# Four low parts move from VectorE to GpSimd: the folded key weights in a three-layer decoder kernel

## The chip, the cores and the metric

The kernel runs on one core of one Trainium2 chip. The metric is device time in microseconds of one execution. A core has five engines with a queue each: TensorE (PE in the profile; its weight loads are the row PEld), VectorE (DVE), ScalarE (ACT), GpSimd (POOL) and SyncE (SP), which here only issues DMAs. GpSimd's operations in this kernel read and write SBUF alone; VectorE and ScalarE also read PSUM, where TensorE's results land.

## The reference

Three layers follow one another on x of 16 x 512 tokens by 256 channels: a linear attention whose state is a product of two summed outer products, a cross attention with 16 heads of 64 channels over 64 context rows per batch entry, and a mixture of eight experts with relu. Each ends in a residual sum and a layer norm. The change lies in the second:

```python
q = x @ Wq.T
kv = context @ Wkv.T
k, v = jnp.split(kv, 2, axis=-1)
...
sim = jnp.einsum('bhid,bhjd->bhij', q, k) * SCALE
...
sim = jnp.where(mask[:, None, None, :], sim, max_neg)
attn = jax.nn.softmax(sim, axis=-1)
out = jnp.einsum('bhij,bhjd->bhid', attn, v)
out = out.transpose(0, 2, 1, 3).reshape(B, Nq, HEADS * DIM_HEAD)
return out @ Wout.T + b_out
```

## The kernel before

After a set-up phase that makes keys and values of all batch entries, the attention phase takes some 900 us and the experts the rest. The change touches the attention phase alone. It walks over 16 batch entries ("batches") with four slots each, one slot per tile of 128 tokens; a steady batch takes 54.9 us. Each engine has its own program for a slot (`pe_slot`, `act_slot`, `dve_slot`, `pool_slot`, `sp_slot`) and runs its instructions strictly in the written order; semaphores, waited for through `need`, are all that ties the engines to each other.

Products that need precision are made in three passes: each operand is held as a rounded high part (`_hi`) and the rest (`_lo`), and `three_passes` multiplies hi by hi, hi by lo, lo by hi.

The key weights of a batch are folded into one matrix A of 256 x 1024 (`a_hi`, `a_lo`): rows are x1's channels, columns the 16 heads times 64 context rows, so that a tile's `sim` is x1 times A. TensorE forms A for the next batch in slot 3 of the present one, in four pieces A0 to A3 of 128 x 512, each in one of two PSUM banks `pw0` and `pw1` that all the small products of a batch share in turn. The table `ORDER` says in which slot and place each is made: A0 and A1 at place a (between the tile's two halves of `sim`), SW at b, A2 at b, A3 at c, SB at d, ROW and M at e. In slot 3 TensorE's sequence is: sim half 0, A0, A1, sim half 1, the transposes of x1 (`tr`), SW, A2, four transposes of the probabilities (`pt`), the product z, A3, four more transposes, those of x, SB, the first half of the output product (`ob`), ROW, M, its second half. Then slot 0 of the next batch begins with sim half 0, which needs all of A.

A name in `SPLIT` is taken out of its bank twice: ScalarE copies it to the high part (`prep_hi`), VectorE subtracts that from the bank to give the low part (`prep_split`), and with this the bank is free. A name in `COPIED` is taken once, by ScalarE (`prep_copied`). `prep_done` picks the semaphore, and `number` its count.

GpSimd makes in each slot the inverse deviations (`rstd`, `nmr`) of the layer norms, adds biases to x1 and x (`xb`), multiplies the probabilities by 1/sum (`prob<-prob,rz`, two halves), and in slot 3 forms the low part of the values, `v_lo`. SyncE writes the mask into row 0 of `a_hi` in slot 0, once A2 is split, since A0 and A2 hold that row.

Of the kernel before, what the change touches and what calls it, by code (L numbers as in the profile page):

```python
# [20 lines left out]
ACT = mybir.ActivationFunctionType  # L21
# [6 lines left out]
P = 128  # L28
# [4 lines left out]
def f32(ap):  # L33
    return ap.bitcast(F32)
# [101 lines left out]
def setup_and_attention(nc, t, k, first, kv_scr, x2_scr, out_rows,  # L136
                        NB, S, C, NKV, MC, TPB, PAIRS, KEYS, HEADS, CAP):
    HK = KEYS // 2
# [44 lines left out]
    s = {n: k.sem(n) for n in (  # L183
        "x_loaded", "k_loaded", "v_loaded",
        "prep_made", "prep_hi", "prep_split", "prep_copied", "state_ready", "st_prod", "r_prod", "r_sum",
        "v_hi_made", "v_lo_made",
        "xT_made", "xT_hi", "xT_taken", "x1T_made", "x1T_hi", "x1T_taken", "xb_ready",
        "z_made", "z_taken", "x1_ready", "x1_biased",
        "sim_made", "max_made", "sim_taken", "exp_made", "sum_made", "rz_made", "p_ready",
# [19 lines left out]

    NAMES = [n for n, _, _ in ORDER]  # L210

    COPIED = ("G", "GT", "R", "SW", "SB")
    SPLIT = ("A0", "A1", "A2", "A3", "B0", "B1", "B2", "B3", "M", "MW", "ROW")
    FINISHED = SPLIT + ("T0", "T1", "ST")

    def number(it, name, kinds=NAMES):

        names = [n for n in NAMES if n in kinds]
        if isinstance(it, int):
            return (sum(enabled(n, i) for i in range(-2, it) for n in names)  # L220
                    + sum(enabled(n, it) for n in names[:names.index(name) + 1]))
        before = sum(enabled(n, i) for i in range(-2, 0) for n in names)
        return it * len(names) + before + names.index(name) + 1
# [4 lines left out]
    def prep_done(eng, it, name):  # L228

        if name in COPIED:  # L230
            need(eng, "prep_copied", number(it, name, COPIED))
        else:
            need(eng, "prep_split", number(it, name, FINISHED))
# [21 lines left out]
    def within(b):  # L255
        return not isinstance(b, int) or 0 <= b < NB

    def need(eng, name, value):

        if not isinstance(value, int) or value > 0:  # L260
            eng.wait_ge(s[name], value)
# [5 lines left out]
    def sp_slot(sp, it, slot, e):  # L267
        if slot == 0 and within(it):

            prep_done(sp, it - 1, "A2")  # L270
            mask_of = maskrow[0:1, it * NKV:(it + 1) * NKV] if isinstance(it, int) else maskrow[0:1, bass.ds(it * NKV, NKV)]
            sp.dma_start(f32(a_hi[0:1, 0, :]).rearrange("p (g j) -> p g j", j=NKV),
                         mask_of.unsqueeze(1).broadcast_to([1, HEADS, NKV])).then_inc(s["mask_in_a"], 16)
        if slot == 0 and within(it + 1):

            if within(it):
                need(sp, "prep_made", number(it - 1, "A3"))
            load_kv(sp, kraw, 0, it + 1, "k_loaded")
        if slot == 1 and within(it + 1):

            need(sp, "v_lo_made", it + 1)
            load_kv(sp, vraw, 1, it + 1, "v_loaded")
        if slot == 3 and within(it + 3):

            need(sp, "xT_made", 4 * (it + 2))
            need(sp, "xb_ready", 4 * (it + 2))
            need(sp, "x_loaded", 16 * (it + 3))
            sp.dma_start(xraw[:, (e + 1) % 2, :, 0:C], x_tiles(it + 3)).then_inc(s["x_loaded"], 16)
        n = 4 * it + slot
        if tile_exists(n - 2):  # L290
            store(sp, n - 2, (slot - 2) % 4, x2, "x2_ready", "x2_stored", x2_scr)
            store(sp, n - 2, (slot - 2) % 4, o_sb, "out_ready", "out_stored", out_rows)
# [129 lines left out]
    def pe_sim(pe, it, slot, h):  # L422

        n = 4 * it + slot
        need(pe, "sim_taken", 2 * n + h - 1)
        if h == 0:
            need(pe, "x1T_taken", n + 1)
            if slot == 0:
                prep_done(pe, it - 1, "A3")
                need(pe, "mask_in_a", 16 * (it + 1))  # L430
        for m in range(MC):
            last = three_passes(pe, sim[h][:, :], (x1T_hi[:, slot, m, :], x1T_lo[:, slot, m, :]),
                                (half(a_hi, h)[:, m, :], half(a_lo, h)[:, m, :]), m == 0, m == MC - 1)
        last.then_inc(s["sim_made"], 1)
# [78 lines left out]
    def prep_views(name):  # L513

        pw = pws[bank_of(name)]
        i = int(name[-1]) if name[-1].isdigit() else 0
        by_m = lambda buf: buf.rearrange("p (m e) -> p m e", m=MC)
        if name == "G":
            return pw[:, 0:2 * C + 2 - P], g_sb[:, :], None
        if name == "GT":  # L520
            return pw[:, 0:P], g10[:, :], None
        if name == "R":
            return pw[:, 0:C], s_bc[:, :], None
        if name == "SW":
            return by_m(pw[:, :]), sw[:, :, :], None
        if name == "SB":
            return by_m(pw[:, 0:MC * P]), sbd[:, :, :], None
        if name == "ROW":
            return pw[0:1, :], rows[0:1, :], rows[32:33, :]
        if name == "M":  # L530
            return by_m(pw[:, :]), mmw_hi[:, :, 0:C], mmw_lo[:, :, 0:C]
        if name == "MW":
            return by_m(pw[:, :]), mmw_hi[:, :, C:2 * C], mmw_lo[:, :, C:2 * C]
        if name[0] == "A":
            return pw[:, :], half(a_hi, i // 2)[:, i % 2, :], half(a_lo, i // 2)[:, i % 2, :]
        return (pw[:, :].rearrange("p (r c) -> p r c", r=2), b_hi[:, 2 * i:2 * i + 2, :],
                b_lo[:, 2 * i:2 * i + 2, :])

    def act_prep(act, name, it):
        if name in COPIED + SPLIT:  # L540
            src, dst, _ = prep_views(name)
            need(act, "prep_made", number(it, name))
            act.activation(dst, src, ACT.Copy).then_inc(s["prep_hi" if name in SPLIT else "prep_copied"], 1)

    def act_norm(act, ln, q, src, dst, done):
# [186 lines left out]
    def pool_rstd(pool, ln, n, q):  # L732

        counted[f"mv{ln}"].wait_next(n + 1)
        pool.tensor_scalar(ve[:, q, ln:ln + 1], mv[:, ln, q, 1:2], EPS, None, ALU.add).then_inc(s[f"ve{ln}"], 1)
        pool.wait_ge(s[f"ve{ln}"], n + 1)

        need(pool, ("z_taken", "x1_ready")[ln], n - 1)
        pool.tensor_tensor(rstd[:, q, ln:ln + 1], ve[:, q, ln:ln + 1], epsc[:, 0:1], ALU.pow).then_inc(s[f"rstd{ln}"], 1)
        if ln:  # L740
            counted[f"rstd{ln}"].wait_next(n + 1)
            pool.tensor_scalar(nmr[:, q, ln:ln + 1], mv[:, ln, q, 0:1], rstd[:, q, ln:ln + 1], -1.0,  # L742
                               ALU.mult, ALU.mult).then_inc(s[f"nmr{ln}"], 1)
# [25 lines left out]
    def pool_state(pool, it):  # L769
# [4 lines left out]
        pool.tensor_tensor(sbdT[:, :, :], sprod[:, :, :], blockmask[:, :].unsqueeze(1).broadcast_to([P, MC, P]),  # L774
                           ALU.mult).then_inc(s["state_ready"], 1)

    def pool_slot(pool, it, slot, e):
        par = lambda a: (e + a) % 2
        has_sim, has_z, has_prev, has_xT, has_x1T = parts(it, slot)
        n = 4 * it + slot  # L780
        q = slot % 2
        if tile_exists(n - 2):
            pool_rstd_twice(pool, n - 2, q)
        if slot == 3 and within(it + 1):
            need(pool, "v_hi_made", it + 2)
            pool.tensor_tensor(v_lo[:, :, :], vraw[:, :, :], f32(v_hi[:, :, :]), ALU.subtract).then_inc(s["v_lo_made"], 1)
        if has_x1T:

            need(pool, "x1T_made", n + 4)
            x1_tile = x1[:, par(1 if slot else 0), (slot - 1) % 4, 1:C + 1]  # L790
            pool.tensor_tensor(x1_tile, x1_tile, boutbc[:, :], ALU.add).then_inc(s["x1_biased"], 1)
        if has_z:
            pool_rstd(pool, 0, n + 4, q)
        if slot == STATE_SLOT and within(it + 2) and not (isinstance(it, int) and it == -2):
            pool_sums(pool, it)
        if has_xT:

            pool_xb(pool, n + 5, it + 1 if slot < 3 else it + 2, (slot + 1) % 4, par(1 if slot < 3 else 2))
        if has_sim:
            need(pool, "rz_made", n + 1)  # L800
            for h in range(2):
                part = by_head(prob[:, q, h * HK:(h + 1) * HK])
                pool.tensor_tensor(part, part, rz[:, q, h * 8:h * 8 + 8].unsqueeze(2).broadcast_to([P, 8, NKV]),  # L803
                                   ALU.mult).then_inc(s["p_ready"], 1)
        if slot == STATE_SLOT and within(it + 2) and not (isinstance(it, int) and it == -2):
            pool_state(pool, it)
        if has_z:
            pool_rstd(pool, 1, n + 4, q)
# [30 lines left out]
    x1T_lo = k.sb("x1T_lo", [P, TPB, MC, P], F32R)  # L839
    a_hi = k.sb("a_hi", [P, MC, KEYS], F32R)  # L840
    a_lo = k.sb("a_lo", [P, MC, KEYS], F32R)
    b_hi = k.sb("b_hi", [P, PAIRS, C], F32R)
    b_lo = k.sb("b_lo", [P, PAIRS, C], F32R)
    v_hi = k.sb("v_hi", [P, PAIRS, P], F32R)
# [750 lines left out]
```

## Time and profile before

| | |
|---|---|
| three runs | 1389.42, 1390.56, 1391.6 us; median 1390.56 |
| the profiled execution | 1389.46 us, its span 1387.7 us |
| busy, share of the span | PE 95%, PEld 84%, DVE 65%, ACT 39%, POOL 44% |
| granted TensorE clock | 0.982 on average, 1.00 in the steady batches |

The profiled execution ends 1.76 us after its span and lies 1.10 us under the median. A timeline row gives the start in us from the start of the span, the duration in us, engine, line, operation, output and inputs; brackets give the engine's idle time ahead of it and what ended that.

### The profile page before, as it was taken

To read this page: it belongs to the slowest core of one execution; us is meant where nothing else is said; L and a number is where in the kernel's file an instruction comes from. 1 tells how busy PE (TensorE), PEld (TensorE's weight loads), DVE (VectorE), ACT (ScalarE), POOL (GpSimd) and SP (SyncE) were. 2 spreads that over 40 slices of the span, in tenths; PEclk is the share of its full clock that TensorE was granted. 3 is DMA by queue.
4 is the path that set the end of the run, shared out by engine and by line. 5 is a ranking of instruction groups with operands and counts; after the bars stand their busy time and mean duration, and the time that the engine had idled before them with its cause. 6 is when DMAs were issued, how large, how long until landed. Compare 5 with 4: busy or idle time off the path is not lost. (4 is left out here: it accounts for less than half of the span.)

```text
span 1387.7 us, 24816 instructions
## 1 busy us (share of the span) xinstructions
PE 1315.2 (95%) x8276; PEld 1161.0 (84%) x8276; DVE 897.2 (65%) x1762; ACT 541.8 (39%) x1041; POOL 604.8 (44%) x958
## 2 busy tenths in 40 slices
PE   7977999999999999999999999898589999999997
PEld 5766888888898888988888988787469988999897
DVE  5535878878878888788788887787434333223333
ACT  2013454454445454544544444344251233213321
POOL 2114656556466466565664665554331221122201
PEclk9999999999999999999999999999989999999999
DMA  8641011111111111111110101310121110111000
GB/s 266 145 97 31 24 39 39 43 35 47 30 46 36 33 46 38 39 38 30 46 45 23 54 32 39 115 31 24 31 62 61 62 36 26 60 60 60 0 0 31
DMA packets 117426, 69.46 MB, mean 50 GB/s; under 512 B 74081, under 2 KB 114786, under 8 KB 117346
## 3 DMA queue, kind: packets, MB, share of 16 engines
q1 hardware_dynamic: 114226, 66.81, 16.5%
q10 hardware_dynamic: 3120, 1.71, 0.4%
q8 instruction: 35, 0.57, 0.2%
q14 instruction: 45, 0.37, 0.1%
HBM read 42.22 MB, written 26.21 MB: 49 GB/s over the span
## 5 line engine op out<-in xcount | busy, mean ns | idle before, releaser
L1378 POOL TENSOR_TENSOR w_lo<-w_raw,w_hi 128x2048 fp32r<-128x2048 f32 x16 | 73.7, 4606 | 241.0 <-ACT w_hi L1329 192.5
L1351 ACT ACTIVATE hT_hi<-up 128x512 fp32r<-128x512 f32 x128 | 76.0, 597 | 236.2 <-PE up L133 236.2
L131 PE MATMUL ob<-b_hi,pT_hi 128*128 128x256 f32 x512 | 160.1, 313 | 6.6 <-DVE pT_lo L728 6.4
L803 POOL TENSOR_TENSOR prob<-prob,rz 128x512 f32<-128x512 f32 x128 | 130.9, 1043 | 66.9 <-DVE rz L690 66.9
L1540 DVE SCALAR_TENSOR_TENSOR hT_lo<-up,hT_hi 128x512 fp32r<-128x512 f32 x128 | 88.3, 691 | 96.6 <-ACT hT_hi L1351 96.6
L131 PE MATMUL dn<-w_hi,hT_hi 128*128 128x256 f32 x512 | 145.3, 284 | 0.8 <-DVE acc L1549 0.8
L133 PE MATMUL ob<-b_hi,pT_lo 128*128 128x256 f32 x512 | 145.2, 284 | 0.0
L133 PE MATMUL dn<-w_hi,hT_lo 128*128 128x256 f32 x512 | 145.1, 283 | 0.0
L132 PE MATMUL dn<-w_lo,hT_hi 128*128 128x256 f32 x512 | 145.1, 283 | 0.0
L132 PE MATMUL ob<-b_lo,pT_hi 128*128 128x256 f32 x512 | 145.1, 283 | 0.0
L547 ACT ACTIVATE x<-h,nmr,rstd 128x256 f32<-128x256 f32 x128 | 76.3, 596 | 116.7 <-POOL nmr L742 109.2
L1549 DVE SCALAR_TENSOR_TENSOR acc<-dn,coef,acc 128x256 f32<-128x256 f32 x64 | 30.9, 484 | 138.4 <-PE dn L133 138.4
L598 ACT ACTIVATE prob<-prob 128x512 f32<-128x512 f32 x128 | 80.7, 630 | 99.0 <-DVE prob L721 99.0
L131 PE MATMUL sim<-a_hi,x1T_hi 128*128 128x512 f32 x256 | 105.5, 412 | 6.1 <-DMA a_hi<-maskrow 6.1
L131 PEld LDWEIGHTS ob<-b_hi,pT_hi 128*128 128x128 f32 x512 | 98.1, 192 | 11.4 <-DVE pT_lo L728 8.0
L131 PE MATMUL up<-x2T_hi,w_hi 128*128 128x512 f32 x256 | 100.9, 394 | 1.5 <-POOL w_lo L1378 1.5
L132 PEld LDWEIGHTS ob<-b_lo,pT_hi 128*128 128x128 f32 x512 | 98.4, 192 | 3.3 <-issue 3.3
L132 PE MATMUL sim<-a_lo,x1T_hi 128*128 128x512 f32 x256 | 101.1, 395 | 0.0
L133 PE MATMUL sim<-a_hi,x1T_lo 128*128 128x512 f32 x256 | 100.6, 393 | 0.0
L132 PE MATMUL up<-x2T_lo,w_hi 128*128 128x512 f32 x256 | 100.5, 393 | 0.0
L133 PE MATMUL up<-x2T_hi,w_lo 128*128 128x512 f32 x256 | 100.3, 392 | 0.0
L131 PEld LDWEIGHTS dn<-w_hi,hT_hi 128*128 128x128 f32 x512 | 98.4, 192 | 1.3 <-DVE acc L1549 1.0
(218 smaller groups left out, 3591.6 us busy)
## 6 DMA issues: line engine op xcount, KB each, us to landing
xraw<-in_x SPq DMA_DIRECT2D x16, 512.0 KB, 4.0
kv_scratch<-stage SPq DMA_DIRECT2D x32, 256.0 KB, 2.6
x_scratch<-x SPq DMA_DIRECT2D x64, 128.0 KB, 1.7
out_x<-o_sb SPq DMA_DIRECT2D x64, 128.0 KB, 1.8
w_raw<-in_L_ffn_experts_inter SPq DMA_DIRECT2D x8, 1024.0 KB, 5.0
w_raw<-in_L_ffn_experts_out SPq DMA_DIRECT2D x8, 1024.0 KB, 7.5
kraw<-kv_scratch SPq DMA_DIRECT2D x32, 128.0 KB, 2.9
vraw<-kv_scratch SPq DMA_DIRECT2D x32, 128.0 KB, 3.0
```

The costliest lines, as they stand in the source:

```text
L131: pe.matmul(out, lh, rh, start=first, stop=False)
L132: pe.matmul(out, lh, rl, start=False, stop=False)
L133: return pe.matmul(out, ll, rh, start=False, stop=last)
L547: act.activation(dst, src, ACT.Identity, bias=nmr[:, q, ln:ln + 1], scale=rstd[:, q, ln:ln + 1]).then_inc(s[done], 1)
L598: act.activation(prob[:, q, h * HK:(h + 1) * HK], prob[:, q, h * HK:(h + 1) * HK], ACT.Exp).then_inc(s["exp_made"], 1)
L803: pool.tensor_tensor(part, part, rz[:, q, h * 8:h * 8 + 8].unsqueeze(2).broadcast_to([P, 8, NKV]), ALU.mult).then_inc(s["p_ready"], 1)
L1351: act.activation(hT_hi[:, h, i, :], up[i % 4][:, :], ACT.Relu).then_inc(s["up_hi"], 1)
L1378: pool.tensor_tensor(lo[:, u, :, :], raw[:, :, :], f32(hi[:, u, :, :]), ALU.subtract).then_inc(s["w_lo_made"], 1)
L1540: dve.scalar_tensor_tensor(hT_lo[:, h, i, :], up[i % 4][:, :], 0.0, f32(hT_hi[:, h, i, :]), ALU.max, ALU.subtract).then_inc(s["up_free"], 1)
L1549: dve.scalar_tensor_tensor(acc[:, i, :], dn[i % 2][:, 0:C], col, acc[:, i, :], ALU.mult, ALU.add).then_inc(s["dn_free"], 1)
```

## The change

A0 to A3 go from `SPLIT` to `COPIED`. ScalarE now reads each bank twice: it makes the high part as before, and right behind it a plain copy in a new SBUF buffer of two places, `a_raw`. GpSimd subtracts the high part from the copy (`pool_a_lo`). GpSimd's four subtractions stand in slot 3: A0 and A1 where `v_lo` stood, A2 between the first norm's `rstd` and `xb`, A3 behind the two multiplications of the probabilities, and `v_lo` behind A3. ScalarE waits ahead of each piece until GpSimd has taken the one before the last (the place in `a_raw`), and TensorE's sim of slot 0 and SyncE's mask wait for `a_lo_made` in place of `prep_split`.

```diff
-    COPIED = ("G", "GT", "R", "SW", "SB")
-    SPLIT = ("A0", "A1", "A2", "A3", "B0", "B1", "B2", "B3", "M", "MW", "ROW")
+    COPIED = ("G", "GT", "R", "SW", "SB", "A0", "A1", "A2", "A3")
+    SPLIT = ("B0", "B1", "B2", "B3", "M", "MW", "ROW")
...
-            prep_done(sp, it - 1, "A2")
+            need(sp, "a_lo_made", 4 * it + 3)
...
-                prep_done(pe, it - 1, "A3")
+                need(pe, "a_lo_made", 4 * (it + 1))
...
-            return pw[:, :], half(a_hi, i // 2)[:, i % 2, :], half(a_lo, i // 2)[:, i % 2, :]
+            return pw[:, :], a_raw[:, i % 2, :], half(a_hi, i // 2)[:, i % 2, :]
...
-            src, dst, _ = prep_views(name)
+            src, dst, hi = prep_views(name)
             need(act, "prep_made", number(it, name))
+            if name[0] == "A":
+                need(act, "a_lo_made", 4 * (it + 1) + int(name[1]) - 1)
+                act.activation(hi, src, ACT.Copy).then_inc(s["a_hi_made"], 1)
             act.activation(dst, src, ACT.Copy).then_inc(s["prep_hi" if name in SPLIT else "prep_copied"], 1)
...
+    def pool_a_lo(pool, it, i):
+
+        need(pool, "a_hi_made", 4 * (it + 1) + i + 1)
+        need(pool, "prep_copied", number(it, f"A{i}", COPIED))
+        pool.tensor_tensor(half(a_lo, i // 2)[:, i % 2, :], a_raw[:, i % 2, :], f32(half(a_hi, i // 2)[:, i % 2, :]),
+                           ALU.subtract).then_inc(s["a_lo_made"], 1)
+
...
-        if slot == 3 and within(it + 1):
-            need(pool, "v_hi_made", it + 2)
-            pool.tensor_tensor(v_lo[:, :, :], vraw[:, :, :], f32(v_hi[:, :, :]), ALU.subtract).then_inc(s["v_lo_made"], 1)
+        has_a = slot == 3 and within(it + 1) and not (isinstance(it, int) and it == -2)
+        if has_a:
+            pool_a_lo(pool, it, 0)
+            pool_a_lo(pool, it, 1)
...
         if has_z:
             pool_rstd(pool, 0, n + 4, q)
+        if has_a:
+            pool_a_lo(pool, it, 2)
...
+        if has_a:
+            pool_a_lo(pool, it, 3)
+            need(pool, "v_hi_made", it + 2)
+            pool.tensor_tensor(v_lo[:, :, :], vraw[:, :, :], f32(v_hi[:, :, :]), ALU.subtract).then_inc(s["v_lo_made"], 1)
```

GpSimd's rows in slot 3 of batch 0, from the last `nmr` of the output norms on, before:

```order
L756 TENSOR_SCALAR nmr<-rstd,mv 128x2
L786 TENSOR_TENSOR v_lo<-vraw,v_hi 128x1024
L791 TENSOR_TENSOR x<-x,boutbc 128x256
L735 TENSOR_SCALAR ve<-mv 128x1
L739 TENSOR_TENSOR rstd<-ve,epsc 128x1
L761 TENSOR_TENSOR xb<-xraw,bprime 128x256
L803 TENSOR_TENSOR prob<-prob,rz 128x512 x2
L735 TENSOR_SCALAR ve<-mv 128x1
L739 TENSOR_TENSOR rstd<-ve,epsc 128x1
L742 TENSOR_SCALAR nmr<-mv,rstd 128x1
```

And after (the line numbers are those of the changed kernel; L784 is `pool_a_lo`):

```order
L759 TENSOR_SCALAR nmr<-rstd,mv 128x2
L784 TENSOR_TENSOR a_lo<-a_raw,a_hi 128x512 x2
L802 TENSOR_TENSOR x<-x,boutbc 128x256
L738 TENSOR_SCALAR ve<-mv 128x1
L742 TENSOR_TENSOR rstd<-ve,epsc 128x1
L784 TENSOR_TENSOR a_lo<-a_raw,a_hi 128x512
L764 TENSOR_TENSOR xb<-xraw,bprime 128x256
L816 TENSOR_TENSOR prob<-prob,rz 128x512 x2
L784 TENSOR_TENSOR a_lo<-a_raw,a_hi 128x512
L821 TENSOR_TENSOR v_lo<-vraw,v_hi 128x1024
L738 TENSOR_SCALAR ve<-mv 128x1
L742 TENSOR_TENSOR rstd<-ve,epsc 128x1
L745 TENSOR_SCALAR nmr<-mv,rstd 128x1
```

`v_lo` has moved behind the multiplications, and four subtractions stand in the queue, one of them between `rstd` and `xb`, one between the multiplications and the next `rstd`.

ScalarE's rows in the same slot, from A0 to the first copy of the transposed probabilities (`pT_hi`), before:

```order
L543 ACTIVATE a_hi<-pw1 128x512
L543 ACTIVATE a_hi<-pw0 128x512
L547 ACTIVATE x1<-h1,nmr,rstd 128x256
L566 ACTIVATE v_hi<-vraw 128x1024
L598 ACTIVATE prob<-prob 128x512
L571 ACTIVATE x1T_hi<-tr 128x256
L543 ACTIVATE sw<-pw1 128x512
L543 ACTIVATE a_hi<-pw0 128x512
L604 ACTIVATE pT_hi<-pt 128x512
```

And after (L545 makes the high part, L546 the plain copy):

```order
L545 ACTIVATE a_hi<-pw1 128x512
L546 ACTIVATE a_raw<-pw1 128x512
L545 ACTIVATE a_hi<-pw0 128x512
L546 ACTIVATE a_raw<-pw0 128x512
L550 ACTIVATE x1<-h1,nmr,rstd 128x256
L569 ACTIVATE v_hi<-vraw 128x1024
L601 ACTIVATE prob<-prob 128x512
L574 ACTIVATE x1T_hi<-tr 128x256
L546 ACTIVATE sw<-pw1 128x512
L545 ACTIVATE a_hi<-pw0 128x512
L546 ACTIVATE a_raw<-pw0 128x512
L607 ACTIVATE pT_hi<-pt 128x512
```

Each `a_hi` is followed by an `a_raw`; x1's norm, `sw` and `pT_hi` stand one to three instructions further back. On VectorE four rows `a_lo<-pw,a_hi` are gone and nothing else moves.

## Rows read from the trace of the kernel before

**Rows 1.** The page's first part: busy time, share of the span, instructions of one engine.
```profile
PE 1315.2 (95%) x8276; PEld 1161.0 (84%) x8276; DVE 897.2 (65%) x1762; ACT 541.8 (39%) x1041; POOL 604.8 (44%) x958
```

**Rows 2.** Waits of PE from 150 to 945 us: total, times, longest.
```profile
PE sim L131 <- DMA a_hi<-maskrow: 6.1, 1, 6.1
PE tr L408 <- ACT x L547: 4.1, 10, 0.4
PE ob L131 <- DVE pT_lo L728: 1.4, 2, 1.3
```

**Rows 3.** Groups of instructions by shape: busy time and mean ns, idle time before.
```profile
L803 POOL TENSOR_TENSOR prob<-prob,rz 128x512 f32<-128x512 f32 x128 | 130.9, 1043 | 66.9 <-DVE rz L690 66.9
...
L1378 POOL TENSOR_TENSOR w_lo<-w_raw,w_hi 128x2048 fp32r<-128x2048 f32 x16 | 73.7, 4606 | 241.0 <-ACT w_hi L1329 192.5 <-ACT w_hi L1332 48.6
...
L614 DVE TENSOR_TENSOR a_lo<-pw,a_hi 128x512 fp32r<-128x512 f32 x64 | 43.7, 690 | 33.4 <-ACT a_hi L543 33.4
...
L786 POOL TENSOR_TENSOR v_lo<-vraw,v_hi 128x1024 fp32r<-128x1024 f32 x16 | 38.1, 2380 | 4.1 <-ACT v_hi L566 4.1
```

**Rows 4.** Timeline of ACT in slot 3 of batch 7; the last row is in slot 0 after it.
```profile
552.78 0.60 ACT L543 ACTIVATE a_hi<-pw 128x512 fp32r<-128x512 f32 x1 [0.30 <-PE pw L389]
553.79 0.60 ACT L547 ACTIVATE x<-h,nmr,rstd 128x256 f32<-128x256 f32 x1 [0.41 <-POOL nmr L742]
...
556.78 0.60 ACT L543 ACTIVATE a_hi<-pw 128x512 fp32r<-128x512 f32 x1 [0.17 <-PE pw L389]
557.27 0.59 ACT L604 ACTIVATE pT_hi<-pt 128x512 fp32r<-128x512 f32 x1
...
560.97 0.41 ACT L543 ACTIVATE sbd<-pw 128x256 f32<-128x256 f32 x1
...
569.28 0.59 ACT L547 ACTIVATE x<-h,nmr,rstd 128x256 f32<-128x256 f32 x1
```

**Rows 5.** Timeline of DVE in the same slot 3.
```profile
558.02 0.68 DVE L728 TENSOR_TENSOR pT_lo<-pt,pT_hi 128x512 fp32r<-128x512 f32 x1
...
559.40 0.18 DVE L647 BATCH_NORM_AGGREGATE mv<-bst 128x2 f32<-128x6 f32 x1
560.37 0.69 DVE L614 TENSOR_TENSOR a_lo<-pw,a_hi 128x512 fp32r<-128x512 f32 x1 [0.79 <-ACT a_hi L543]
...
562.30 0.25 DVE L690 RECIPROCAL rz<-zsum 128x16 f32<-128x16 f32 x1
```

**Rows 6.** Timeline of POOL in the same slot 3 and the slot after it.
```profile
555.28 0.27 POOL L756 TENSOR_SCALAR nmr<-rstd,mv 128x2 f32<-128x2 f32 x1 [0.19 <-POOL rstd L754]
555.51 2.38 POOL L786 TENSOR_TENSOR v_lo<-vraw,v_hi 128x1024 fp32r<-128x1024 f32 x1
...
559.75 0.22 POOL L735 TENSOR_SCALAR ve<-mv 128x1 f32<-128x1 f32 x1 [1.27 <-DVE mv L647]
...
560.59 0.74 POOL L761 TENSOR_TENSOR xb<-xraw,bprime 128x256 f32<-128x256 f32 x1
562.64 2.04 POOL L803 TENSOR_TENSOR prob<-prob,rz 128x512 f32<-128x512 f32 x2 [1.30 <-DVE rz L690]
...
565.83 0.27 POOL L742 TENSOR_SCALAR nmr<-mv,rstd 128x1 f32<-128x1 f32 x1 [0.19 <-POOL rstd L739]
```

**Rows 7.** Timeline of PE in the same slot 3: x1's transposes, ROW.
```profile
554.53 0.41 PE L408 MATMUL tr<-ident,x 128*128 128x128 f32 x2 [0.41 <-ACT x L547]
...
561.83 0.61 PE L366 MATMUL pw<-sbd,bq 128*128 128x128 f32 x4
```

**Rows 8.** Timeline of PEld: the first weight load of the next batch's slot 0.
```profile
565.35 0.19 PEld L131 LDWEIGHTS sim<-a_hi,x1T_hi 128*128 128x128 f32 x1
```

**Rows 9.** Timeline of PE in slots 0 of batches 14 and 15.
```profile
899.85 0.77 PE L131 MATMUL sim<-a_hi,x1T_hi 128*128 128x512 f32 x1 [6.10 <-DMA a_hi<-maskrow]
...
949.80 0.40 PE L131 MATMUL sim<-a_hi,x1T_hi 128*128 128x512 f32 x1
```

**Rows 10.** Timeline of POOL in slot 3 ahead of batch 15.
```profile
947.75 2.05 POOL L803 TENSOR_TENSOR prob<-prob,rz 128x512 f32<-128x512 f32 x2 [2.05 <-DVE rz L690]
```

More of the change, by code:

```diff
@@ L185, in setup_and_attention @@
         "prep_made", "prep_hi", "prep_split", "prep_copied", "state_ready", "st_prod", "r_prod", "r_sum",
-        "v_hi_made", "v_lo_made",
+        "v_hi_made", "v_lo_made", "a_hi_made", "a_lo_made",
         "xT_made", "xT_hi", "xT_taken", "x1T_made", "x1T_hi", "x1T_taken", "xb_ready",
@@ L841, in setup_and_attention @@
     a_lo = k.sb("a_lo", [P, MC, KEYS], F32R)
+    a_raw = k.sb("a_raw", [P, 2, HK])
     b_hi = k.sb("b_hi", [P, PAIRS, C], F32R)
```

## Prediction

> **What bounds the kernel now.** I read the page's busy shares first: PE is busy 95% of the span and DVE 65% [rows 1]. Then the waits of PE between 150 and 945 us, where the steady batches lie: the reader is to see how little is there. One wait of 6.1 us is for the mask of batch 14, which queues behind the experts' first weights; the rest is 4.1 us at x1's transposes and 1.4 us for VectorE's `pT_lo` [rows 2]. In 795 us PE stands still for 5.5 us besides the mask. So TensorE's stream is the bound, and VectorE, which the change relieves, holds it up for 1.4 us of it. A change of the copy engines can give back hardly anything, and it costs whatever it makes TensorE wait. The question is therefore one of due times in slot 3: which of the new instructions end after TensorE asks for them. I follow slot 3 of batch 7 (549 to 565 us); its rows repeat from batch to batch within some 0.1 us.
>
> TensorE asks for A at the first weight load of slot 0, at 565.35 [rows 8]. Before, VectorE had A3's low part done at 560.37 + 0.69 = 561.06 [rows 5], well ahead. Now it comes from GpSimd, and behind two multiplications that ended at 564.68 [rows 6].
>
> **What goes.** Four subtractions of 0.69 us on VectorE per batch [rows 3], 2.76 us. They lie under TensorE's work, so I cost their absence at nothing. What gets earlier is the softmax's chain: the reciprocal `rz` stood at 562.30 to 562.55 [rows 5], 1.24 us behind the end of A3's subtraction (the sum over the probabilities lies between). Now that sum can start at about 559.8, when the statistics of z are done (below), and `rz` is there near 559.8 + 1.24 + 0.25 = 561.3. GpSimd waited 1.30 us for it ahead of the multiplications [rows 6]; that gap is the cover for the new work, and it is used up below.
>
> **What ScalarE adds.** Four plain copies per batch. Two of its operations in a row start 0.49 us apart: A2's `a_hi` at 556.78 and `pT_hi` at 557.27 [rows 4]. The trace has no second copy of a bank, but this one waits for nothing, so 0.49 us is its price; the bounds are 0.49 and the full 0.60. The copy of A0 falls into the idle 0.30 us ahead of A1 and moves A1 by 0.09; A1's copy moves x1's norm, which waited 0.41 us for `nmr`, from 553.79 to 551.88 + 4 x 0.49 = 553.84 [rows 4]. TensorE waits for that norm already [rows 7], so this passes on: 0.05 to 0.06 us. A2's copy moves `pT_hi` by 0.55 to 557.82, A3's moves `sbd` by 0.55 from 560.97 to 561.52, done 561.93 [rows 4]; ROW's matmuls at 561.83 [rows 7] need it and start some 0.2 us late. This 0.2 is not added to the sum, because TensorE then waits that much less at slot 0.
>
> `pT_hi` ends at 558.41, so VectorE's `pT_lo`, at 558.02 before, starts at 558.46 and ends near 559.1. Behind it stands the statistics of z, and its aggregate of 559.40 [rows 5] becomes 559.62. GpSimd's `ve` waits for just that and goes from 559.75 to 559.97 [rows 6]. The subtraction that left VectorE from ahead of `pT_lo` gives nothing back, since the new copy on ScalarE is the longer way.
>
> **What GpSimd adds.** The trace has no 128x512 subtraction there. Rows of the same operation with two full inputs are 2.380 us for 1024 columns and 4.606 for 2048 [rows 3]: 2.17 ns a column and 0.15 us fixed, so 512 columns take 1.26 to 1.27. The bounds are 1.04, the 512 columns of `prob` whose second input is only 16 numbers wide over both halves [rows 3], and 1.48, twice the 0.74 of `xb` [rows 6]. I take 1.25. Operations in a row start 0.04 before the end of the one ahead, as `v_lo` and `nmr` show [rows 6].
>
> A0 and A1 take the place of `v_lo`, from 555.51: 2 x 1.25 against 2.38, over by 557.97. Then x1's bias, and GpSimd is waiting for z at 559.97 as before. Then:
>
> - `ve` to `xb` was 0.84 us [rows 6]: A2 starts at 560.81 and ends 562.06;
> - `xb` 562.02 to 562.76; the multiplications 562.72 to 564.76, against 564.68 before: A2 has used the 1.30 us of cover, and nothing is left for A3;
> - A3 564.72 to 565.97; with 0.05 for the semaphore TensorE may load at 566.02 instead of 565.35: 0.67 us of wait per batch.
>
> The Trainium skill, page "GPSIMD Engine Reference", section 4.1 "Engine selection", speaks against this step: elementwise work on a tile belongs on VectorE, GpSimd being about twice as slow with two inputs. Its section 3.1 gives 4497 ns for 2048 columns, where this trace has 4606 for a subtraction of that size. Taking a quarter, 1.12 us, as an estimate from that page, the wait would be about 0.4 and the sum 7 us; the rows above decide.
>
> What is queued behind A3: `v_lo` (2.38) and the norm that gives x1's `nmr`, whose end was 1.42 us after the multiplications' [rows 6]. With the 0.04 of overlap it comes 2.34 + 1.42 = 3.76 us after A3's end, at 569.73. x1's norm in slot 0 was at 569.28, 3.93 us after TensorE's start on that slot [rows 4, 8], as it stands behind MW on ScalarE; with the shift it is at 569.95. So this second wait is covered, by 0.2 us. SyncE's mask goes out when A2's low part is there, 562.1 in place of 560.4, and is needed at 566: covered.
>
> **The sum.** A is made in slot 3 of batches 0 to 14 and once ahead of batch 0. For 13 of them (made for batches 1 to 13) 0.67 each: 8.7 us. For batch 14 TensorE waits 6.10 us for the mask anyway [rows 9] and A3 is hidden; the weights that hold the mask up are issued behind a store that ScalarE's norms release, 0.55 later: 0.5. For batch 15 the multiplications end at 949.80 [rows 10], just when TensorE starts sim [rows 9]: 1.3. For batch 0 there are no multiplications, GpSimd is later all the same: 0.4, between 0 and 1. Together 10.9 us. The profiled execution took 1389.46, so 1400.4; the median of the runs is 1.10 above it, so 1401.5. I say 1401.
>
> **The rivals.**
> *Hidden or nearly so.* If a subtraction costs 1.04 (the lower bound), A3 ends 0.42 earlier, and if `pT_lo` does not hold up the statistics, another 0.22: 0.03 to 0.25 per batch, 1 to 4 us with the edges: 1391.5 to 1395. For it: the row of `prob` is of this very size. Against: both its inputs are not full tiles.
> *ScalarE becomes the bound.* It now also waits for GpSimd: A2's `a_hi` needs A0's place in `a_raw`, free at 555.51 + 1.25 = 556.76, and was made at 556.78 before [rows 4, 6]: no slack. If GpSimd is later by some tenths, `a_hi`, `pT_hi` and `pT_lo` follow, and TensorE's second four transposes, which need the bank that `pT_lo` reads, and ROW wait with them. With 1.48 per subtraction alone the wait at slot 0 is 0.67 + 2 x 0.23 = 1.13 per batch; with an estimated 0.3 on top, the size of the delays on ScalarE, it is 1.4: 1389.5 + 18 + 2 + 1, 1410 or more.
> *Faster.* VectorE's 2.76 us per batch come ahead of everything that feeds TensorE, the waits for `pT_lo` and for x1's norm shrink, and A3 is hidden by the lower bound. All there is to win is the 4.1 + 1.4 us of [rows 2] and some in the last slots: 1384 to 1387. It would decide from the point where A3's low part ends before 565.3. Against it: x1's norm in slot 3 waits for GpSimd's `nmr`, whose queue VectorE's relief, later in that slot, does not reach.
>
> **How the numbers follow.** My forecast (0.4 to 1.1 us per batch, 1395.5 to 1408) gets 0.62, for its order of work is fixed and only one price is unknown. Hidden or nearly so 0.20, of which 0.12 lies within 0.2% (2.8 us, 1387.8 to 1393.3, about what a measurement can tell) and 0.08 above. ScalarE as bound 0.08. Faster 0.10, of which 0.02 within 0.2%. So faster 0.08, same 0.14, slower 0.78. The range of 8 in 10 goes from 1392, which takes in the upper part of the hidden case, to 1408, the upper bound of the price.
>
> **What would show it.** Right: a wait of PE or PEld at sim's first load in slot 0 for POOL `a_lo` of about 0.5 to 0.7 us, some 13 times; `a_lo<-a_raw,a_hi` at 1.25; the multiplications in slot 3 with no wait for `rz`; VectorE 44 us less busy, ScalarE 30 to 38 more, GpSimd 80 more. Wrong: `a_lo` near 1.04 or below and no wait at sim; waits that move to `pt` or ROW for ScalarE; or x1's transposes waiting in slot 0 for `nmr` by more than before, since its cover is 0.2 us.

## The result, and the profile after

The changed kernel takes 1405.93 us (median of 4 runs, 1405.35 to 1406.84) against 1389.99 us before (4 runs, 1388.78 to 1391.6): a ratio of 1.0115, 95% interval 1.0097 to 1.0132. It is slower by 15.9 us, where the forecast had added 10.9 us and named 1401. The measured time lies inside the range of 1392 to 1408, in its upper part. Its profiled execution took 1405.35 us, with a span of 1403.6.

The page's first part answers to [rows 1]:

```profile
PE 1320.2 (94%) x8276; PEld 1159.9 (83%) x8276; DVE 861.8 (61%) x1698; ACT 568.2 (40%) x1105; POOL 683.1 (49%) x1022
```

VectorE is busy 35 us less, ScalarE 26 and GpSimd 78 more, and TensorE 5 us more in a span 16 us longer. The waits of PE between 150 and 960 us (total, times, longest), which answer to [rows 2]:

```profile
PE tr L408 <- ACT x L550: 7.8, 15, 0.6
PE sim L131 <- DMA a_hi<-maskrow: 6.5, 1, 6.5
PE sim L131 <- POOL a_lo L784: 3.1, 12, 0.4
PE ob L131 <- DVE pT_lo L731: 1.3, 1, 1.3
```

A new wait has come, for `a_lo` at the first sim of a batch, 12 times, and that for x1's norm at the transposes has grown from 4.1 to 7.8 us. The wait for `pT_lo`, which is VectorE's, has hardly moved, 1.4 to 1.3. These rows understate what is lost. In batch 7 the first sim shows a wait of 0.29 us on PE, and its row lasts 0.49 us where that of before lasts 0.40:

```profile
573.87 0.49 PE L131 MATMUL sim<-a_hi,x1T_hi 128*128 128x512 f32 x1 [0.29 <-POOL a_lo L784]
```

With the wait at x1's transposes (0.54 us after 0.41) the rows list 0.42 us more than before, while the slot became 0.95 us longer, as follows. So the distance between weight loads is the better measure. The groups that answer to [rows 3]:

```profile
L784 POOL TENSOR_TENSOR a_lo<-a_raw,a_hi 128x512 fp32r<-128x512 f32 x64 | 81.7, 1287 | 0.9 <-ACT a_raw L546 0.7 <-ACT a_hi L545 0.2
...
L546 ACT ACTIVATE a_raw<-pw 128x512 f32<-128x512 f32 x64 | 38.5, 601 | 0.0
...
L821 POOL TENSOR_TENSOR v_lo<-vraw,v_hi 128x1024 fp32r<-128x1024 f32 x16 | 38.2, 2389 | 0.0
```

Now batch 7 again. PEld's rows, where slot 3 begins (the first load of sim), x1's transposes, ROW, and the beginning of slot 0:

```profile
556.86 0.19 PEld L131 LDWEIGHTS sim<-a_hi,x1T_hi 128*128 128x128 f32 x1
...
562.20 0.20 PEld L408 LDWEIGHTS tr<-ident,x 128*128 128x128 f32 x2 [0.93 <-issue]
...
569.68 0.52 PEld L366 LDWEIGHTS pw<-sbd,bq 128*128 128x128 f32 x4 [0.20 <-ACT sbd L546]
...
573.87 0.19 PEld L131 LDWEIGHTS sim<-a_hi,x1T_hi 128*128 128x128 f32 x1 [0.49 <-issue]
```

Slot 3 lasts 573.87 - 556.86 = 17.01 us. Before, the rows of the same loads were these, with the end of the slot in [rows 8]:

```profile
549.29 0.19 PEld L131 LDWEIGHTS sim<-a_hi,x1T_hi 128*128 128x128 f32 x1
...
554.50 0.20 PEld L408 LDWEIGHTS tr<-ident,x 128*128 128x128 f32 x2 [0.80 <-issue]
...
561.72 0.53 PEld L366 LDWEIGHTS pw<-sbd,bq 128*128 128x128 f32 x4
```

That is 565.35 - 549.29 = 16.06 us, so this slot 3 costs 0.95. Counted from the start of the slot, x1's transposes come at 5.34 us, where they came at 5.21 before. ROW's first load comes at 12.82 after 12.43, later by 0.39, of which 0.13 stem from the transposes and 0.26 are new. The next sim comes at 17.01. ScalarE's rows, to be held against [rows 4]:

```profile
560.99 0.62 ACT L546 ACTIVATE a_raw<-pw 128x512 f32<-128x512 f32 x1
561.47 0.62 ACT L550 ACTIVATE x<-h,nmr,rstd 128x256 f32<-128x256 f32 x1
...
564.55 0.60 ACT L545 ACTIVATE a_hi<-pw 128x512 fp32r<-128x512 f32 x1 [0.25 <-PE pw L389]
565.05 0.59 ACT L546 ACTIVATE a_raw<-pw 128x512 f32<-128x512 f32 x1
565.53 0.61 ACT L607 ACTIVATE pT_hi<-pt 128x512 fp32r<-128x512 f32 x1
...
569.21 0.42 ACT L546 ACTIVATE sbd<-pw 128x256 f32<-128x256 f32 x1
...
577.77 0.59 ACT L550 ACTIVATE x<-h,nmr,rstd 128x256 f32<-128x256 f32 x1
```

VectorE's, against [rows 5]:

```profile
566.17 0.69 DVE L731 TENSOR_TENSOR pT_lo<-pt,pT_hi 128x512 fp32r<-128x512 f32 x1 [1.89 <-ACT pT_hi L607]
...
567.32 0.18 DVE L650 BATCH_NORM_AGGREGATE mv<-bst 128x2 f32<-128x6 f32 x1
...
568.73 0.25 DVE L693 RECIPROCAL rz<-zsum 128x16 f32<-128x16 f32 x1
```

and GpSimd's, against [rows 6]:

```profile
562.85 0.27 POOL L759 TENSOR_SCALAR nmr<-rstd,mv 128x2 f32<-128x2 f32 x1 [0.19 <-POOL rstd L757]
563.08 2.52 POOL L784 TENSOR_TENSOR a_lo<-a_raw,a_hi 128x512 fp32r<-128x512 f32 x2
...
567.68 0.22 POOL L738 TENSOR_SCALAR ve<-mv 128x1 f32<-128x1 f32 x1 [1.49 <-DVE mv L650]
...
568.52 1.29 POOL L784 TENSOR_TENSOR a_lo<-a_raw,a_hi 128x512 fp32r<-128x512 f32 x1
569.76 0.73 POOL L764 TENSOR_TENSOR xb<-xraw,bprime 128x256 f32<-128x256 f32 x1
570.44 2.06 POOL L816 TENSOR_TENSOR prob<-prob,rz 128x512 f32<-128x512 f32 x2
572.44 1.29 POOL L784 TENSOR_TENSOR a_lo<-a_raw,a_hi 128x512 fp32r<-128x512 f32 x1
573.69 2.39 POOL L821 TENSOR_TENSOR v_lo<-vraw,v_hi 128x1024 fp32r<-128x1024 f32 x1
...
577.11 0.27 POOL L745 TENSOR_SCALAR nmr<-mv,rstd 128x1 f32<-128x1 f32 x1 [0.19 <-POOL rstd L742]
```

The last subtraction ends at 573.73 and sim's load follows at 573.87. GpSimd has not one gap from `rstd` to that end: the wait of 1.30 us for `rz` is gone, as `rz` (568.73) is there long before the multiplications (570.44).

The same distance taken for each of the 64 slots gives a table that all experiments are read in. It is worked out from the start rows of these loads; each entry is the median over batches 2 to 11, and within a kernel most of the distances lie within 0.1 us of it (slot 0 scatters by up to 0.3). The four entries of before add up to 54.8 us a batch, not 54.9.

| kernel | slot 0 | slot 1 | slot 2 | slot 3 |
|---|---|---|---|---|
| before | 13.85 | 14.11 | 10.78 | 16.06 |
| after | 13.79 | 14.11 | 10.77 | 16.99 |
| A3 early | 14.09 | 14.11 | 10.77 | 16.46 |
| VectorE subtracts in SBUF | 13.86 | 14.11 | 10.77 | 16.49 |
| A3 twice | 13.80 | 14.11 | 10.78 | 18.34 |
| A1 twice | 13.79 | 14.11 | 10.77 | 16.99 |
| A3 early, v_lo last | 13.85 | 14.12 | 10.77 | 16.46 |
| before, norm first | 13.85 | 14.11 | 10.77 | 15.54 |
| A3 early, v_lo last, norm first | 13.88 | 14.11 | 10.77 | 16.46 |
| only A0 and A1 moved | 13.85 | 14.11 | 10.77 | 16.20 |

At the first sim of the last slot the changed kernel's profiled execution is 15.9 us behind that of before. The delay builds up like this (after less before): 1.5 us up to the first sim of batch 0, 12.5 in the slots 3 of batches 0 to 12, -0.9 in the slots 0 up to batch 13, 1.0 in slot 3 of batch 13, where the mask is waited for, -0.7 in batch 14, 1.5 in its slot 3, 1.0 in batch 15. The experts' phase behind it takes the same time.

### The profile page after: what moved, and what is told of

It reads as the page before. It is cut to its first block and busy times, and to the rows that moved or that the text cites. A ratio compares the mean times of both kernels' runs of the same rounds, so it can differ in the third digit from the quotient of the medians.

```text
span 1403.6 us, 24971 instructions
## 1 busy us (share of the span) xinstructions
PE 1320.2 (94%) x8276; PEld 1159.9 (83%) x8276; DVE 861.8 (61%) x1698; ACT 568.2 (40%) x1105; POOL 683.1 (49%) x1022
## 5 line engine op out<-in xcount | busy, mean ns | idle before, releaser
L731 DVE TENSOR_TENSOR pT_lo<-pt,pT_hi 128x512 fp32r<-128x512 f32 x128 | 86.0, 672 | 46.3 <-ACT pT_hi L607 44.9
L719 DVE TENSOR_REDUCE mx<-sim 128x8 f32<-128x512 f32 x128 | 88.3, 689 | 38.4 <-PE sim L133 37.9
L738 POOL TENSOR_SCALAR ve<-mv 128x1 f32<-128x1 f32 x128 | 28.5, 222 | 165.2 <-DVE mv L650 164.4
```

The lines of the kernel that those rows point to most:

```text
L719: dve.tensor_reduce(mx[:, h * 8:h * 8 + 8], by_head(sim[h][:, :]), AX.X, ALU.max).then_inc(s["max_made"], 1)
L731: dve.tensor_tensor(pT_lo[:, h * 4:h * 4 + 4, :], pt[:, :].rearrange("p (r u) -> p r u", u=P), f32(pT_hi[:, h * 4:h * 4 + 4, :]), ALU.subt ...
```

## The experiments

The first four kernels were measured together with 7 runs of the kernel before (median 1389.28 us), the last four with 10 runs of it (median 1389.15). Each ratio is against the kernel before of the same set.

### The due time of A3, and what ScalarE adds

Three theories could make 16 us. Theory 1, the forecast's: GpSimd delivers A3's low part too late. Theory 2: it is ScalarE's copies. Theory 3: GpSimd's 78 us of new work slow others down wherever they stand.

**A3 early.** GpSimd's subtraction for A3 goes ahead of the multiplications:

```diff
+        if has_a:
+            pool_a_lo(pool, it, 3)
         if has_sim:
             need(pool, "rz_made", n + 1)
...
         if has_a:
-            pool_a_lo(pool, it, 3)
             need(pool, "v_hi_made", it + 2)
```

> The changed kernel, with GpSimd's subtraction for A3 ahead of the two multiplications of the probabilities instead of behind them; nothing else. Theory 1 (the due time of A3's low part in GpSimd's queue costs TensorE's wait at the start of slot 0): the wait for a_lo at sim is gone. What is left per batch is 0.13 us at x1's transposes and 0.26 us at ROW in slot 3, both from ScalarE, and up to 0.2 us at x1's transposes in slot 0, because nmr comes no earlier while TensorE does: 0.4 to 0.6 us per batch above the kernel before, 1397 to 1400 us in all, 6 to 9 below the changed kernel. Theory 2 (ScalarE's four extra copies cost the time, wherever GpSimd stands): 1404 to 1406, no change. Theory 3 (GpSimd's added work slows others through shared access to SBUF, wherever it stands): no change either.

Measured: 1402.65 us (1401.83 to 1403.71), ratio 1.0101 (1.0084 to 1.0118). In the table slot 3 is where theory 1 put it, 0.40 above before (0.39 expected) and 0.53 below after, and slot 0, at 14.09, has lost 0.24 (up to 0.2 expected). The wait at sim for `a_lo` is gone. Yet the whole came out 3 us above the expectation's upper end. The steady slots give 7.6 us, as expected; 2.0 more lie ahead of batch 0 and 3.3 in batch 15, and the expectation had no term for these. Theory 1 rests on the slots here: by the whole time alone, 3.3 us below the change, it could hardly be told from theory 2.

**VectorE subtracts in SBUF.** ScalarE as in the change, GpSimd as before:

```diff
-        if name in SPLIT:
+        if name[0] == "A":
+            pool_a_lo(dve, it, int(name[1]))
+        elif name in SPLIT:
             src, hi, lo = prep_views(name)
```

> ScalarE as in the changed kernel (high part and plain copy), but VectorE subtracts in SBUF from the plain copy, in its old places, and GpSimd is as before. Theory 1: only ScalarE's share is left, 0.13 us at x1's transposes plus 0.26 at ROW per batch, 0.4 us, or 1395 to 1397 us in all. Theory 2: 1404 to 1406, as the extra copies are all there. Theory 3: near 1395 as well, so it is told from theory 1 by the fourth kernel of this set, not by this one.

Measured: 1400.7 us (1398.84 to 1402.48), ratio 1.008 (1.006 to 1.0099). Slot 3 is at 16.49: 0.43 us for ScalarE's copies, with GpSimd's queue as before, where 0.4 was expected. Theory 2 falls as the whole cause and stands for a part. The total is some 4 us above what was expected, and this too lies at the edges: 1.9 ahead of batch 0, 1.0 in slot 3 of batch 13, 2.5 in that of batch 14.

**A3 twice, A1 twice.** The same extra subtraction at two places in GpSimd's queue:

```diff
+        if twice:
+            pool.tensor_tensor(half(a_lo, i // 2)[:, i % 2, :], a_raw[:, i % 2, :],
+                               f32(half(a_hi, i // 2)[:, i % 2, :]), ALU.subtract).then_inc(s["again"], 1)
+            need(pool, "again", it + 2)
```

> The changed kernel, with A3's subtraction made twice, one waiting for the other: 1.29 + some 0.15 us more in GpSimd's queue between the multiplications and the release of sim, 16 times. Theory 1: all of it is TensorE's wait, 1.44 us in each of 15 batches and less or nothing where the mask is waited for: 20 to 23 us more, 1426 to 1429. Theory 2: 0 to 3 us more, as ScalarE does nothing new. Theory 3: a quarter of what GpSimd's 64 subtractions cost, some 4 us: 1410.

> The changed kernel, with A1's subtraction made twice: the same work as in the kernel with A3 twice, but where GpSimd afterwards waits 1.49 us for the statistics of z. Theory 1: 0 to 2 us more (1406 to 1408), since the wait takes up 1.44 us. Theory 3: the same 4 us as with A3 twice, since the amount is the same. Theory 2: no change.

Measured: A3 twice 1425.36 us (1423.76 to 1426.48), ratio 1.0261 (1.0243 to 1.0278); A1 twice 1404.25 (1403.47 to 1404.34), ratio 1.011 (1.0093 to 1.0127), against 1.0115 for the change. Both came out below what theory 1 had expected in all, 1426 to 1429 and 1406 to 1408, A1 twice by nearly 2 us. But the same work costs some 20 us at one place and nothing at the other: slot 3 goes to 18.34, by 1.35, or stays at 16.99. PE's wait at sim with A3 twice:

```profile
PE sim L131 <- POOL a_lo L788: 20.8, 13, 1.8
```

And GpSimd's rows with A1 twice, where the third subtraction and x1's bias end at 566.55 and `ve` can start right after:

```profile
562.06 1.28 POOL L788 TENSOR_TENSOR a_lo<-a_raw,a_hi 128x512 fp32r<-128x512 f32 x1
563.29 1.30 POOL L785 TENSOR_TENSOR a_lo<-a_raw,a_hi 128x512 fp32r<-128x512 f32 x1
564.66 1.29 POOL L788 TENSOR_TENSOR a_lo<-a_raw,a_hi 128x512 fp32r<-128x512 f32 x1
565.92 0.63 POOL L806 TENSOR_TENSOR x<-x,boutbc 128x256 f32<-128x256 f32 x1
566.66 0.22 POOL L738 TENSOR_SCALAR ve<-mv 128x1 f32<-128x1 f32 x1
```

`ve` starts 4.60 us behind the start of the first subtraction (562.06), exactly as after the change (567.68 and 563.08). The gap of 1.49 us ahead of it has shrunk to 0.1, and nothing is later. So theory 3 falls: this much more work on GpSimd is free where it fills a gap, and the place behind the multiplications is what costs. Theory 1 holds for the loss per batch.

### What is queued behind A3, and ScalarE's share taken apart

**A3 early, v_lo last.** As A3 early, with `v_lo` behind `pool_rstd(pool, 1, n + 4, q)`, the norm that gives x1's `nmr`.

> As the kernel with A3 early, and v_lo moved behind GpSimd's last norm of slot 3, so that x1's nmr comes 2.4 us sooner. The kernel with A3 early had a slot 3 of 16.46 us and a slot 0 of 14.10, where the kernel before has 16.06 and 13.85. Theory (the 0.25 us in slot 0 are a wait for nmr, put off by v_lo; the 0.40 us in slot 3 are ScalarE's): slot 0 is back at 13.85, slot 3 stays at 16.46; in all 1396 to 1399. Rival (slot 0 is longer because the multiplications or x1's bias come later): slot 0 stays at 14.1, in all 1401 to 1403.

Measured: 1398.39 us (1397.11 to 1400.8), ratio 1.007 (1.0054 to 1.0087). Slot 0 is back at 13.85. In the profile 5.4 of the 8.9 us above before lie in batches 0 to 12 and 3.5 at the edges. In the kernel with A3 early GpSimd's `v_lo` and `nmr` stood so:

```profile
572.37 2.39 POOL L822 TENSOR_TENSOR v_lo<-vraw,v_hi 128x1024 fp32r<-128x1024 f32 x1
...
575.78 0.27 POOL L745 TENSOR_SCALAR nmr<-mv,rstd 128x1 f32<-128x1 f32 x1 [0.19 <-POOL rstd L742]
```

and ScalarE, which makes x1 in slot 0, had this:

```profile
575.43 0.60 ACT L546 ACTIVATE mmw_hi<-pw 128x512 fp32r<-128x512 f32 x1 [3.96 <-PE pw L380]
576.16 0.60 ACT L550 ACTIVATE x<-h,nmr,rstd 128x256 f32<-128x256 f32 x1
```

x1's norm starts 0.73 us behind MW's `mmw_hi` instead of 0.49, because `nmr` ends at 576.05. In the change itself this is hidden by the later sim: x1 at 577.77 is right behind MW, with `nmr` done at 577.38. This is the second wait that the forecast named.

**Only A0 and A1 moved.** A2 and A3 are back in `SPLIT`.

> Only A0 and A1 are moved as in the change; A2 and A3 are taken out as in the kernel before, and v_lo stands where the change has it. Theory (ScalarE's 0.40 us in slot 3 are 0.13 at x1's transposes, from the copies of A0 and A1, and 0.27 at ROW, from the copies of A2 and A3): slot 3 at 16.15 to 16.25, slot 0 at 13.85, PE waits for no a_lo; 1391 to 1394 us in all. Rival (the 0.40 us come with the first two copies alone, the delay being handed on): slot 3 at 16.4 to 16.5, 1396 to 1398.

Measured: slot 3 at 16.20, 0.14 above before. So ScalarE's 0.40 is 0.14 at x1's transposes, from the copies of A0 and A1, and 0.26 at ROW, from the copies of A2 and A3. In all 1397.44 us (1394.02 to 1398.74), ratio 1.0058 (1.0039 to 1.0076): 8.3 us above before, of which batches 0 to 12 explain 2. The expectation of 1391 to 1394 had no term for the edges: in the profile 2.5 lie ahead of batch 0, 1.6 in slot 3 of batch 13 and 1.3 in batch 15.

**Before, norm first.** In the kernel before, TensorE waited 0.4 us for x1's norm in slot 3 of most batches [rows 2, 7], and in GpSimd's queue of slot 2 the two products of the state stood ahead of it. They change places:

```diff
+        if has_z:
+            pool_rstd(pool, 1, n + 4, q)
         if slot == STATE_SLOT and within(it + 2) and not (isinstance(it, int) and it == -2):
             pool_state(pool, it)
-        if has_z:
-            pool_rstd(pool, 1, n + 4, q)
```

> The kernel before, with one thing changed: in slot 2 GpSimd makes x1's rstd and nmr ahead of the two products of the state, not behind them. Theory: TensorE's wait at x1's transposes in slot 3 (0.41 us on PE, 0.80 on PEld) is for nmr in GpSimd's queue; nmr comes 1.6 us sooner, then ScalarE's A1 copy is the next limit and TensorE's weight load can start 0.4 to 0.5 us sooner: slot 3 goes from 16.06 to 15.6 in the ten batches that have this wait, 1384 to 1387 us in all. Rival (the state's products, 1.4 us later, hold up SW): slot 3 stays or grows, 1389 or more.

Measured: 1384.23 us (6 runs, 1382.8 to 1385.7) against 1389.15 in its set, ratio 0.9969 (0.9956 to 0.9981). Slot 3 is at 15.54, 0.52 below before. GpSimd's `nmr` and the first product of the state:

```profile
548.62 0.27 POOL L742 TENSOR_SCALAR nmr<-mv,rstd 128x1 f32<-128x1 f32 x1 [0.19 <-POOL rstd L739]
548.84 0.73 POOL L772 TENSOR_TENSOR sprod<-s 128x256 f32<-128x256 f32 x1
```

and ScalarE's A1 and x1:

```profile
549.78 0.60 ACT L543 ACTIVATE a_hi<-pw 128x512 fp32r<-128x512 f32 x1 [0.29 <-PE pw L389]
550.27 0.59 ACT L547 ACTIVATE x<-h,nmr,rstd 128x256 f32<-128x256 f32 x1
```

x1's norm follows A1's high part after 0.49 us, no longer `nmr`. This version is faster than both kernels, that of before by 4.9 us.

**The same with the change** (A3 early, v_lo last, norm first):

> The kernel with A3 early and v_lo last, plus the same earlier norm in slot 2 as in the kernel before with the norm first. Theory (with the change it is ScalarE's copies of A0 and A1, four operations in a row of 0.49 us, that set x1's norm in slot 3, no longer nmr): nothing is gained, slot 3 stays at 16.4 to 16.5 and the whole within 1 us of the kernel without the earlier norm. Rival (nmr still sets it): slot 3 falls by 0.4 as in the other, 4 us less in all.

Measured: 1396.97 us (1395.57 to 1398.17), ratio 1.0061 (1.0045 to 1.0076), 1.4 us below the kernel without the earlier norm, a difference inside the spread of both. Slot 3 stays at 16.46. `nmr` is there early:

```profile
556.23 0.26 POOL L745 TENSOR_SCALAR nmr<-mv,rstd 128x1 f32<-128x1 f32 x1 [0.19 <-POOL rstd L742]
```

but ScalarE is still making A1's plain copy when it could start on x1:

```profile
558.02 0.62 ACT L546 ACTIVATE a_raw<-pw 128x512 f32<-128x512 f32 x1
558.50 0.62 ACT L550 ACTIVATE x<-h,nmr,rstd 128x256 f32<-128x256 f32 x1
```

The difference expected was at most 1 us. So the change has a second price that its own trace does not show: with the norm first, slot 3 is 15.54 without the change and 16.46 with it, 0.92 us a batch instead of 0.40. The two kernels also differ in GpSimd's subtractions, but x1's norm stands right behind ScalarE's copy in these rows, so the price is put down to the copies. The wait for `nmr` had hidden 0.52 of it.

## Why the prediction came out as it did

**The bound and the sign: right.** TensorE's stream is what counts, VectorE's 2.76 us per batch gave nothing back (its wait went from 1.4 to 1.3 us), and A3's low part is late at sim. The forecast's 5.5 us of waits left out a row of the same view, 0.9 us at `pt` for `pT_lo`; it is 0.9 us after the change as well. The experiments show A3's low part as the cause of the steady loss: 0.53 us per batch are gone when A3 stands ahead of the multiplications, and a second subtraction behind them costs in full. The 0.40 that then remain are ScalarE's on TensorE's own path. In the change they are not added to the 0.95, because TensorE reaches sim before A3 does; ScalarE's copies enter there through `pT_hi` and `ve` instead, with 0.36 of the 0.95.

**The size per batch: too small, 0.67 against 0.95 in batch 7.** The chain is the one forecast, each link a little longer, counted from the slot's start as in the forecast:

- `ve` came 0.36 us later than before, not 0.22. It starts 10.82 us into the slot (567.68), 10.46 before. ScalarE's copies of A0 and A1 delay x1's transposes by 0.13, not 0.06, and A2's `a_hi` and then `pT_hi` follow: `pT_hi` is at 8.67, after 7.98 before, later by 0.69 and not by 0.55. This is 0.14 of the miss. A2's `a_hi` is itself later by 0.20, which is 0.07 more than the transposes are. That is not the wait for the place in `a_raw` that the second rival feared: where VectorE subtracts, and that place is free 3 us sooner, A2's `a_hi` comes 7.74 us into the slot, against 7.71 after the change (medians). Where the 0.07 come from is open.
- From `ve` to the end of A3 it took 573.73 - 567.68 = 6.05, not 6.00. A subtraction is 1.29, not 1.25, the multiplications and `xb` as before: 0.05.
- From that end to sim's load passed 0.14, not 0.05: 0.09. The 0.05 had no row behind it. In the changed kernel's trace this distance alternates between 0.05 in the even and 0.13 to 0.14 in the odd batches from 2 to 10, and slot 3 with it between 16.95 and 17.01, so for half of the batches the 0.05 was right.

0.67 + 0.14 + 0.05 + 0.09 = 0.95. The price of a subtraction, on which the range was built, was nearly right; what was mis-sized is the delay that ScalarE's copies hand on through `pT_hi` and the statistics. The Trainium skill's figure ("GPSIMD Engine Reference", section 3.1 "Elementwise — side-by-side cycle accounting", a quarter of 4497 ns, an estimate) would have been 1.12 us and too short against the measured 1.29; the line through this kernel's own rows was the better source.

That the whole time stayed inside the range is partly luck: the upper bound of 1408 stood for a dearer subtraction, and that room was used up by the delay behind ScalarE's copies and by the edges.

**The busy times: smaller changes than forecast on two engines.** GpSimd's 78 us more meet the 80 of the forecast. VectorE is 35 us less busy, not 44, and ScalarE 26 more, not 30 to 38, though the groups of subtractions that went (43.7 us) and of copies that came (38.5 us) have the sizes forecast. Rows of operations in a row overlap by some 0.11 us on ScalarE (565.05 + 0.59 against 565.53), which an engine's busy time counts once; how much of the two differences this makes was not worked out.

**Taken as hidden, and hidden: ROW's delay.** It is 0.26 us (forecast 0.2) and shows only in kernels without the wait at sim. The cover of 1.30 us for A2's subtraction held too, and x1's norm in slot 0 was covered, by 0.39 us and not 0.2.

**The edges: too small, 2.2 forecast against 4.3.** What comes ahead of batch 0, 0.4 in the forecast, was 1.5. Slot 3 of batch 13, 0.5 in the forecast, was 1.0. Its mechanism was right, that the store puts off the mask, by 0.88 us and not by 0.55: the first load for the experts goes out 11.11 us into the slot, after 10.23 before (the row of before is at 888.02, its slot began at 877.79):

```profile
901.99 0.40 SPq L79 DMA_DIRECT2D acc<-x_scratch  x1
```

Slot 3 of batch 14, 1.3 in the forecast, was 1.5. The remaining 0.3 are a gain and a loss in slots that make no A (-0.7 in batch 14 and 1.0 in batch 15). Batch 15 differs from kernel to kernel by several us (from -0.6 to 3.3 against before) in ways that no run was made to explain, so that part of each total is located and stays open.

**The steady sum: too small, 8.7 forecast for 13 batches against 12.5 in their slots 3, less 0.9 in the slots 0.** The excess of 3.8 in the slots 3 is the 0.28 per batch of above, 13 times; batches 0, 1 and 12, whose slot 3 was 15.7 us before and not 16.06, lost 1.0 to 1.2. The forecast had no term for the gain in the slots 0. It goes with the wait at sim and not with VectorE's relief: slot 0 is 13.79 or 13.80 in the three kernels that wait there for `a_lo`, and 13.85 with A3 early and `v_lo` last, where VectorE is relieved too. Steady sum and edges together are 11.6 + 4.3 = 15.9.

## What to carry to other kernels

In this kernel the work that moved to an engine with idle time cost by its due time, not by its length. To see this ahead of a run, follow that engine's queue from the last event it waits for to the first instruction that waits for it, and ask what stands ahead. The same subtraction was free ahead of a gap and cost its whole length behind the multiplications. The engine that made the extra copy for the move paid as well, on what stood behind the copy; another wait covered half of this, and it showed only once that other wait was gone. A sum of steady batches also needs terms for the start and the end: here the edges held 4.3 of 15.9 us.

## What the runs showed that was not expected

**The clock ahead of batch 0.** The start of the attention phase differs with the granted clock. The stretch 121 to 125 us, which holds TensorE's work after a wait of 3.3 us for VectorE, was at these clocks before, after, and with A1 twice (busy us of each engine, then PEclk):

```profile
121.00:125.00 4.00, 4.00 (x19) 3.46 (x18) 0.57 (x2) 1.84 (x4) 2.95 (x2) 0.68 0.02 4
```

```profile
121.00:125.00 4.00, 4.00 (x16) 3.54 (x15) 0.42 (x1) 1.57 (x4) 1.81 (x2) 0.50 0.02 4
```

```profile
121.00:125.00 4.00, 4.00 (x18) 3.50 (x17) 0.42 (x1) 2.12 (x5) 3.19 (x4) 0.68 0.01 4
```

At 0.50, the 1.2 GHz level, all through the stretch, the changed kernel's execution came 1.5 us late to batch 0; at 0.68 the kernel with A1 twice, with the same edits and more, came 0.4 late. All ten kernels fall in two groups: before, norm first without the change, and A1 twice have 0.68 to 0.70 and reach batch 0 within -0.2 to 0.4 us of before; the other seven have 0.50 and reach it 1.5 to 3.4 us late. The same work of TensorE, from the start of A's third group of matmuls to that of its fourth, took 2.94 us before (122.72 to 125.66), 2.83 with A1 twice (122.90 to 125.73) and 3.98 after the change (122.80 to 126.78). So about 1 us of the difference between the two profiled executions goes with this clock. It is not all: three of the kernels at 0.50 come 2.0 to 3.4 us late, which no run explains. Whether ScalarE's copies make the lower level likelier (seven of the eight kernels that have them) or it is chance in single executions is open.

**A subtraction on VectorE with both inputs in SBUF and GpSimd's operations hold each other up.** This shows in the kernel in which VectorE subtracts in SBUF, in slot 3 of batch 7:

```profile
561.57 2.38 POOL L799 TENSOR_TENSOR v_lo<-vraw,v_hi 128x1024 fp32r<-128x1024 f32 x1
563.68 0.82 DVE L786 TENSOR_TENSOR a_lo<-a_raw,a_hi 128x512 fp32r<-128x512 f32 x1 [1.12 <-ACT a_raw L546]
563.92 1.08 POOL L804 TENSOR_TENSOR x<-x,boutbc 128x256 f32<-128x256 f32 x1
```

VectorE's subtraction for A2 begins while GpSimd's `v_lo` still runs and takes 0.82 us, where 44 of the 64 subtractions of this kernel take 0.68 or 0.69. It ends 0.55 us behind the end of `v_lo`, and in the other batches it is longer in the same way by what is left of `v_lo`. GpSimd's bias addition, which then starts beside it, takes 1.08 us, where it takes 0.63 to 0.74 in the kernel before. There the same subtraction for A2, with one input in the bank, ran beside `v_lo` for 0.48 us (from 557.41 to 557.89) and still took 0.69. So the third theory had something real behind it, but not where it looked. In the change itself these subtractions are off VectorE, GpSimd's all take 1.27 to 1.31 us, and a second subtraction for A1 on GpSimd made no slot longer. In this kernel too it costs TensorE at most 0.03 us a batch (slot 3 at 16.49 against 16.46).
